# A four-block modulated convolution chain: V's low parts, w3's rounding and the filter copies rearranged

## The reference

```
for k in range(4):
    x = x + block(x, cond_512, weights[k], biases[k], mod_w[k], mod_b[k])
# block: four layers, 'same', 'upsample', 'same', 'downsample'
s = style @ mw.T + mb
weight = SCALE * w * s[:, None, :, None]
demod = rsqrt(sum(weight * weight, axis=(2, 3)) + EPS)
weight = weight * demod[:, :, None, None]
```

## Time and profile before

| | |
|---|---|
| median of 3 runs | 1401.16 us (1399.49 to 1403.38) |
| the profiled execution | 1402.98 us |
| its span, first to last instruction | 1401.2 us |
| TensorE busy | 1325.6 us, 95% |
| VectorE, ScalarE, GpSimd busy | 1101.9, 784.6, 327.1 us |
| mean granted TensorE clock | 0.987 of full |
| DMA | 257.51 MB |
| filter copies, gh and gl | 254 + 254 DMAs of 224 KB |

### The profile page before, as it was taken

How to read it: one execution, slowest core, us unless ns; L and a number is a source line. 1 busy time by engine, 2 the same in 40 slices (tenths; PEclk the granted TensorE clock), 3 DMA queues, 4 the chain that set the end, 5 groups by cost and what they waited for, 6 DMA issues and landing times.

```text
span 1401.2 us, 20330 instructions
## 1 busy us (share of the span) xinstructions
PE 1325.6 (95%) x6565; PEld 1085.8 (77%) x6565; DVE 1101.9 (79%) x1792; ACT 784.6 (56%) x1465; POOL 327.1 (23%) x632
## 2 busy tenths in 40 slices
PE   7799999999999999999999999999999999999998
PEld 5587877787888788788788777788787777777776
DVE  6788788887787878888787788888787667778764
ACT  5556465655555555555555555555556466665663
POOL 2213211132213212114122211213212232222210
PEclk9899999999999999999999999999999989999999
DMA  8457867677876658877766867677865497687664
GB/s 298 117 122 195 210 177 193 167 186 204 219 188 174 168 162 219 211 183 199 168 190 185 218 175 197 148 187 205 225 184 155 106 182 192 175 220 189 180 165 114
DMA packets 148201, 257.51 MB, mean 184 GB/s; under 512 B 14784, under 2 KB 81344, under 8 KB 148096
## 3 DMA queue, kind: packets, MB, share of 16 engines
q1 hardware_dynamic: 147728, 255.93, 70.9%
q10 hardware_dynamic: 368, 0.28, 0.1%
HBM read 72.39 MB, written 67.24 MB: 100 GB/s over the span
## 4 chain that ended last, share of the span: by engine, by line
PE 41%; DVE 23%; ACT 10%; issue 9%; DMA 7%; SPq 7%; POOL 2%; ACTq 0%; DVEq 0%; POOLq 0%
PE ps L463 40%; DMA gl<-sl 7%; DVE zl L978 4%; SPq L343 4%; ACT kp L750 4%; SPq L344 3%; DVE gf L1029 3%; DVE xl L972 3%; DVE X L987 3%; ACT xh L709 2%; DVE vl L1015 2%; DVE v L1013 2%; DVE vf L1008 1%; DVE vh L1017 1%; DVE gf L1035 1%
## 5 line engine op out<-in xcount | busy, mean ns | idle before, releaser
L463 PE MATMUL ps<-zh,gh 128*128 128x512 f32 (+1 forms) x1028 | 410.8, 400 | 9.9 <-DMA gh<-sh 4.5
L463 PE MATMUL ps<-zl,gh 128*128 128x512 f32 (+1 forms) x1028 | 407.7, 397 | 0.0
L721 ACT ACTIVATE zh<-ps,t_bx 128x512 fp32r<-128x512 f32 x256 | 176.2, 688 | 315.0 <-PE ps L463 312.8
L463 PE MATMUL ps<-zh,gl 128*128 128x512 f32 (+1 forms) x1028 | 285.0, 398 | 17.5 <-DMA gl<-sl 17.2
L750 ACT ACTIVATE kp<-ps,t_T1s 64x256 f32<-64x256 f32 x512 | 213.0, 464 | 157.6 <-PE ps L463 154.4
L987 DVE SCALAR_TENSOR_TENSOR X<-ps,t_D,X 128x512 f32<-128x512 f32 x255 | 190.2, 746 | 94.8 <-PE ps L463 73.7
L978 DVE SCALAR_TENSOR_TENSOR zl<-ps,t_bx,zh 128x512 fp32r<-128x512 f32 x256 | 191.1, 746 | 88.7 <-ACT zh L721 85.1
L972 DVE SCALAR_TENSOR_TENSOR xl<-X,t_S,xh 128x513 fp32r<-128x513 f32 x256 | 190.8, 765 | 78.5 <-ACT xh L709 77.2
L463 PEld LDWEIGHTS ps<-zh,gl 128*128 128x128 f32 x1028 | 191.2, 189 | 71.7 <-DMA gl<-sl 29.5
L463 PEld LDWEIGHTS ps<-zh,gh 128*128 128x128 f32 x1028 | 196.3, 191 | 60.6 <-issue 8.0
L463 PEld LDWEIGHTS ps<-zl,gh 128*128 128x128 f32 x1028 | 196.0, 191 | 45.2
(11 more groups left out here) (204 smaller groups left out, 1583.0 us busy)
## 6 DMA issues: line engine op xcount, KB each, us to landing
out_x<-X SPq DMA_DIRECT2D x255, 256.5 KB, 6.6
gh<-sh SPq DMA_DIRECT2D x254, 224.0 KB, 3.9
gl<-sl SPq DMA_DIRECT2D x254, 224.0 KB, 4.4
X<-out_x SPq DMA_DIRECT2D x96, 513.0 KB, 8.3
X<-x_in SPq DMA_DIRECT2D x32, 513.0 KB, 9.1
pk<-taps_in SPq DMA_DIRECT2D x3, 512.0 KB, 11.9
pk<-pack_in SPq DMA_DIRECT2D x3, 352.0 KB, 11.2
pk<-sets_in SPq DMA_DIRECT2D x4, 256.0 KB, 9.0
```

What stands on the lines that cost most here:

```text
L463: return pe.matmul(out_ap, a, b, start=first, stop=last, skip_group_check=True)
L721: act.activation(zh[n % 2][:, ZPAD:ZPAD + M], ps[:, ZP + n % 2, :], IDENT, bias=tab["bx"][:, k, b:b + 1]).then_inc(s["zhi"], 1)
```

## The change

Four edits, in three parts.

- `vlo` goes from the end of VectorE's iteration 3 to its front, ahead of xlo, xnew and zlo.
- `w3hi` goes from the end of ScalarE's iteration 3 to the front of iteration 0.
- `sh` and `sl` get an eighth tap slot, set to zero by two memsets on GpSimd at the start. A partition's filters of a pair, 2 samples by 8 slots by 64 channels, are then one run of 4096 B. The copy to the lower half takes the run whole; the copy to the upper half takes its first 3840 B and writes them one slot (256 B) further, so that the first sample's zero slot becomes the second sample's slot 0. Before, each partition's copy was two runs of 1792 B.

```
-        sh = sb("sh", [128, 2, NT, C], F32R)
-        sl = sb("sl", [128, 2, NT, C], F32R)
+        sh = sb("sh", [128, 2, NT + 1, C], F32R)
+        sl = sb("sl", [128, 2, NT + 1, C], F32R)
...
         def by_tap(a):
-            return a.rearrange("p i t c -> p t i c")
+            return a[:, :, 0:NT, :].rearrange("p i t c -> p t i c")
+
+        def flat(a):
+            return a.rearrange("p i t c -> p (i t c)")
...
-                        src = of[rows, :, :, :].bitcast(F32)
-                        sp.dma_start(to[0:C, h % 3, :, 0:NT, :].bitcast(F32), src).then_inc(s[name], 16)
-                        sp.dma_start(to[C:128, h % 3, :, 1:NT + 1, :].bitcast(F32), src).then_inc(s[name], 16)
+                        src, dst = flat(of[rows]).bitcast(F32), flat(to[:, h % 3]).bitcast(F32)
+                        sp.dma_start(dst[0:C, :], src).then_inc(s[name], 16)
+                        sp.dma_start(dst[C:128, C:], src[:, 0:PAIR - C]).then_inc(s[name], 16)
...
             for n in range(2, NN):
+                if v_at(n + 1) is not None and n + 1 not in V_LATE:
+                    w3hi(v_at(n + 1))
                 if n + 3 < NN:
                     xhi(n + 3)
...
-                if v_at(n + 2) is not None:
-                    w3hi(v_at(n + 2))
...
             for n in range(2, NN):
                 due = g_at(n - 1)
+                if v_at(n - 2) is not None and n - 2 not in V_LATE:
+                    vlo(v_at(n - 2))
                 if due is None and n + 3 < NN:
                     xlo(n + 3)
                 xnew(n - 1)
...
-                if v_at(n - 2) is not None and n - 2 not in V_LATE:
-                    vlo(v_at(n - 2))
...
+            for a in (sh, sl):
+                link(pool.memset(a[:, :, NT, :].bitcast(F32), 0.0))
```

More of the change, by code:

```diff
@@ L57 @@
 KS = 10
+PAIR = 2 * (NT + 1) * C
 EVEN, ODD, CORR, NONE = slice(1, 8, 2), slice(2, 8, 2), 0, 9
```

## The result

The changed kernel takes 1418.72 us in the median of 4 runs (1417.57 to 1422.36) against 1401.01 for the kernel before, a ratio of 1.013 (95% interval 1.011 to 1.015). It is slower by 17.7 us, where 13 were forecast. The profiled execution took 1418.13 us, its span is 1416.3.

A forecast was written before the change was run, and what follows sets the result against it. TensorE was taken as the bound, raced by V's low parts and the gl copies. Terms of +16.5, -4.3, +0.2 and +0.7 us sum to +13, giving 1414 us, range 1376 to 1436.

The forecast's parts named there:

- What bounds the kernel: TensorE, 95% busy, raced by V's low parts and filter copies; without K waits it wants gl half a microsecond early.
- the term for the V waits: TensorE's waits for V's low parts before the K products, removed over 62 groups: 44.8 us by start times.
- the sum: Per group, gl's landing + 0.66 us against TensorE's want without V waits, old V and gl waits taken off: +13 us.
- Part 1: vlo at the front of VectorE's iteration 3 ends before the K products start; V waits go, 44.8 us.
- Part 2: w3's rounding on ScalarE, order changing only in the last block: zero, bounds -1 to +1 us.
- Part 3, the price by bytes: SP's filter copies cost by bytes, +0.91 us, less 0.25 for sooner first issue: last gl landing +0.66 (+0.4 to +0.95).
- Rivals 1 and 2: Filter copies: half the rows, about half the time, 1337 us, chance 0.10; or longer rows offset their bytes, 1378, 0.14.
- 33 regular groups: Groups of blocks 0 to 2: V and gl waits go from 33.7 to 50.2 us, +16.5.
- 19 groups with edge work: Groups with edge or setup work, gl wanted at 11.0 us: waits go from 12.4 to 8.1 us, -4.3.
- 10 of the last block: Last-block groups, gl landing at 10.92 and wanted at 9.83 us: waits go from 17.7 to 17.9 us, +0.2.
- Rival 3: vlo on VectorE still waits for ScalarE's rounding or GpSimd's w3 work; K waits stay: +25 us, 1426, chance 0.15.
- The signs named beforehand: TensorE's V waits under 5 us, gl over 60; some 12 MB more; about 226 GB/s; issue 0.35 us; group 20.9 us.

The follow-up runs named there:

- part 4: Kernel before with vlo first and four 128-partition DMAs per group for eight, half the filters wrong: 1320.38 us; the same with vlo last: 1377.99 us.
- part 3 of the experiments: Against the kernel with vlo first: copies of 256 KB, same number of rows, 1480.72 us; copies of 224 KB in half the rows, leaving work out, 1359.31 us.
- experiment 1: Kernel before with only vlo moved to the front of VectorE's iteration 3: 1386.83 us, and 1384.4 us when repeated with more rounds.
- the kernel of 1550.56 us: Kernel before with six DMA copies per group for eight, ScalarE copying the high parts' own halves, vlo last: 1550.56 us (1.105).

## Why the prediction was right, point by point

- **What bounds the kernel**: two chains with half a microsecond between them. The changed kernel shows the second alone, and the pair with and without slow copies (part 4) shows that each hid the other. Alone, the term for the V waits was too large: the sum had 23 us for vlo first on the old copies and 12 on the new ones, measured are 14 to 16 and 6. The forecast of 13 for both together came within 5 us of 17.7.
- **Part 1**: the V waits fell by 43.5 us by start times (44.8 to 1.3), 44.8 forecast. That vlo would end before K held. It runs in 1.6 us where I allowed 2.8.
- **Part 2**: nothing, as forecast.
- **Part 3, the price by bytes**: +0.66 us for the chain, measured +0.65 in the median (10.45 to 11.10) and +0.67 in the mean. That it is met so closely is in part luck: the two pieces are each a little off and make up for each other. The seven landings after the first take 0.67 us longer, where bytes alone give 0.76; the first copy's issue fell to 0.47 us and not to 0.34, and its first landing was 0.25 us earlier only where the bytes stayed (2.74 against 2.99 us); in the changed kernel, with 256 KB, the first landing is 2.94. The prediction took the Trainium skill's rule on coalescing (DMA: Bandwidth & Descriptors, Rules for kernel authors) as one on rows. It is one on whole transfers, under 64 KB, and a copy here is 224 KB, so it speaks for neither rival. Rivals 1 and 2 fall with part 3 of the experiments: the bytes alone make a copy longer, and halving the rows alone leaves it as it was.
- **The sum**, by start times in the trace of the changed kernel: 51.1 us of V and gl waits in the 33 regular groups (50.2 forecast), 13.9 in the 19 groups with edge work (8.1), 14.0 in the 10 of the last block (17.9). Together 79.0 in place of 63.9, 15.1 us more. That the span grew by the same 15.1 us is in part chance, since these are the V and gl waits alone, without the last group and without the wait for gh told below.
- **What was mis-sized**: the groups with edge work, and 5.2 of their 5.8 us in three groups for which the sum had no new wait: they wait 1.3, 1.1 and 2.8 us. I took the time at which TensorE wants gl there from the trace of before with the V wait taken off, 11.6 to 12.0 us after the chain began. But in these groups TensorE also ran at half its clock behind the V wait. TensorE's timeline in one of them, and the busy-time view of the stretch (columns as above), both of the kernel before:

```profile
1143.35 1.22 PE L463 MATMUL ps<-vl,w1h 128*128 128x256 f32 x4 [3.33 <-DVE vl L1015]
```

```profile
1143.00:1149.60 6.60, 6.25 (x19) 5.24 (x20) 2.89 (x5) 3.40 (x8) 0.39 (x2) 0.51 1.08 198
```

  With the V waits gone the half clock behind them went as well. TensorE came earlier, at 9.8, 10.4 and 9.2 us, and gl kept it longer. The same term explains a part of what is missing in experiment 1, where the groups with edge work wait 7.2 us and the sum had 1.0, 3.9 of it in the same three. The rest there lies in landings that come later than before, in the last block 11.1 to 11.4 us in the mean in place of 10.9, which I did not take further.
- **One group that the sum had not**: at the start of the last block the copies meet the stores of X of many samples at once, issued at 1162 to 1165. The landing of the first copy (KB, us), and TensorE's timeline:

```profile
gh<-sh SPq DMA_DIRECT2D x1, 256.0 KB, 8.3
```

```profile
1182.68 0.47 PE L467 MATMUL ps<-zh,gh 128*128 128x512 f32 x1 [4.20 <-issue]
1186.97 2.07 PE L467 MATMUL ps<-zh,gl 128*128 128x512 f32 x4 [1.19 <-DMA gl<-sl]
```

  The first copy took 8.3 us to land, gl landed after 16.6 us, and TensorE stood 4.2 and 1.2 us and ran at half clock for 6.8 us from 1183 on. The sum's statement that gh never binds fails in this one group.
- **Rival 3** fell: no V wait is left, in spite of the 0.01 us between the two engines. vlo ends 1.8 us before the K products in the regular group shown, so a late start by some tenths would cost nothing.
- **The signs named beforehand**: gl waits over 60 us (70.8), V waits under 5 (0.4), 12 MB more (12.5), the rate kept (228), a regular group 20.9 to 21.1 us. The issue time alone missed (0.47, not 0.35).

## What to carry to other kernels

Where a transfer touches only one half of the partitions, count its bytes and not its rows: padding rows to make them whole cost 7 to 14% of each copy here and bought 0.13 us of SP's first issue. Whole rows without more bytes were worth 25 to 27 us, in good part by an earlier first landing (2.74 against 2.99 us). When a wait is taken away, compute from the same group when the next chain ends; a 34 us wait gave 14 us because a DMA stood half a microsecond behind it, and once that was quick the same edit gave 58. Look at the granted clock too before you take a time from a trace: behind a long wait it can hold half clock that goes with the wait. The cheapest copy is the one not made: an engine that already holds the data on the right partitions can write it where it belongs, if nothing that TensorE waits for stands behind it on that engine.

## What the runs showed of the hardware

- DMAs inside SBUF that read 64 partitions and write 64 ran at 218 to 233 GB/s (214 to 218 by their landings) with rows of 1792 to 4096 B; the same rows of 1792 B over 128 partitions ran at 371 GB/s.
- Long waits of TensorE can cost more than their own length. In the kernel of 1550.56 us TensorE stood 2.46 us until 246.98, and then got half its clock (1.2 of 2.4 GHz) for 3.4 us. Its timeline, and then the busy-time view of the stretches after it (third column from the end: granted clock):

```profile
246.98 0.58 PE L469 MATMUL ps<-vl,w1h 128*128 128x256 f32 x1 [2.46 <-DVE vl L1037]
```

```profile
247.00:250.20 3.20, 3.20 (x11) 2.91 (x12) 1.79 (x3) 1.31 (x4) 0.00 (x0) 0.50 1.00 131
251.00:271.00 20.00, 18.25 (x90) 15.13 (x89) 14.96 (x26) 11.46 (x19) 1.47 (x2) 0.99 0.69 204
```

  Not every such wait brings it: in that trace, from 80 us on, TensorE waited 51 times for 1.7 us or more, and with 39 of these waits a stretch at half clock began, during the wait or up to 1.8 us after its end. Of the 40 such stretches there only the one at the kernel's end began without one. Its mean clock is 0.942, that of the kernel with more bytes 0.968, of the others 0.984 to 0.992.
- VectorE's vl instruction took 1.11 us beside GpSimd's w3 work (L1015 in the kernel before, the group of rows 8) and 0.69 us ahead of it (L1019 in the changed kernel). Over the whole trace of before it took 1.10 us in the mean in 46 cases beside a GpSimd instruction and 0.69 in the 18 others.
